# Second-half score blocks issued on the neighbouring array tiles, in turn with those of the first half

## What is computed

```python
scores = jnp.einsum('bhqd,bhkd->bhqk', q, k) / math.sqrt(D_HEAD)
scores = jnp.where(causal, neg_inf, scores)
vals, idx = jax.lax.top_k(scores, K_S)
masked = jnp.put_along_axis(jnp.full_like(scores, -jnp.inf), idx, vals, axis=-1, inplace=False)
out = jnp.einsum('bhqk,bhkd->bhqd', jax.nn.softmax(masked, axis=-1), v)
...
h = jax.nn.relu(jnp.einsum('edi,bsi->bsed', proj_in, x))
o = jnp.einsum('eid,bsed->bsei', proj_out, h)
return jnp.einsum('bsei,bse->bsi', o, gate)
...
xq = _quantize_activations(x @ H)
return jnp.einsum('bsi,oi->bso', xq, _ternary_quantize_ste(weight))
```

## Time and profile before

| | us |
|---|---|
| median of 3 runs | 622.53 |
| lowest, highest | 621.35, 623.42 |
| profiled execution, own time | 624.53 |
| its span | 622.7 |
| PE busy in the span | 553.3 (89%) |
| DVE busy | 477.5 (77%) |
| ACT busy | 387.2 (62%) |
| POOL busy | 344.3 (55%) |

### The profile page before, as it was taken

How to read it: one execution, slowest core, us unless ns; L and a number is a source line. 1 busy time by engine, 2 the same in 40 slices (tenths; PEclk the granted TensorE clock), 3 DMA queues, 4 the chain that set the end, 5 groups by cost and what they waited for, 6 DMA issues and landing times. The chain is left out here.

```text
span 622.7 us, 20334 instructions
## 1 busy us (share of the span) xinstructions
PE 553.3 (89%) x7156; PEld 478.9 (77%) x7156; DVE 477.5 (77%) x2995; ACT 387.2 (62%) x909; POOL 344.3 (55%) x336
## 2 busy tenths in 40 slices
PE   4565648999899999999999999999999999989942
PEld 3454537898788888888888888888888888878831
DVE  1898879986889978898879887988789898553213
ACT  3688558666567566766667576766575767646520
POOL 2488556753447464754556455655554656555831
PEclk9568578999999999999999999999999999999985
DMA  7244220001000200002000100020001000000000
GB/s 234 78 146 136 86 103 2 3 17 37 3 2 3 64 8 2 3 3 69 3 1 21 53 3 2 3 70 1 3 3 53 3 3 1 19 0 3 18 0 17
DMA packets 20021, 19.88 MB, mean 32 GB/s; under 512 B 1744, under 2 KB 17872, under 8 KB 19920
## 3 DMA queue, kind: packets, MB, share of 16 engines
q1 hardware_dynamic: 19920, 18.59, 9.6%
HBM read 16.49 MB, written 2.10 MB: 30 GB/s over the span
## 5 line engine op out<-in xcount | busy, mean ns | idle before, releaser
L462 POOL TENSOR_TENSOR h_lo<-h_raw,h_hi 128x512 f16<-128x512 f32 x128 | 149.5, 1169 | 158.9 <-ACT h_raw L580 158.2
L768 PE MATMUL ps_o<-w_hi,h_lo 128*128 128x256 f16 x512 | 139.8, 273 | 4.3 <-POOL h_lo L462 3.1
L752 PE MATMUL ps_z<-x1t_hi,w_lo 128*128 128x256 f16 x512 | 140.5, 274 | 0.6 <-DVE x1t_lo L910 0.6
L752 PE MATMUL ps_z<-x1t_lo,w_hi 128*128 128x256 f16 x512 | 140.3, 274 | 0.0
L752 PE MATMUL ps_z<-x1t_hi,w_hi 128*128 128x256 f16 x512 | 140.3, 274 | 0.0
L768 PE MATMUL ps_o<-w_hi,h_hi 128*128 128x256 f16 x512 | 139.5, 273 | 0.0
L768 PE MATMUL ps_o<-w_lo,h_hi 128*128 128x256 f16 x512 | 139.5, 273 | 0.0
L854 DVE MATCH_REPLACE8 taken<-next,taken 128x48 f32<-128x48 f32 (+2 forms) x576 | 127.6, 233 | 0.2
L576 ACT ACTIVATE h_hi<-ps_z 128x512 f16<-128x512 f32 x128 | 75.9, 593 | 57.9 <-PE ps_z L752 57.0
L849 DVE MAX8 next<-taken 128x8 f32<-128x48 f32 (+2 forms) x576 | 95.9, 235 | 0.1
L483 POOL TENSOR_TENSOR acc<-go_sb,acc 128x512 f32<-128x512 f32 x56 | 71.2, 1271 | 36.4 <-ACT go_sb L590 36.2
(11 more groups left out here) (106 smaller groups left out, 993.5 us busy)
## 6 DMA issues: line engine op xcount, KB each, us to landing
w_raw<-in_w1t SPq DMA_DIRECT2D x8, 512.0 KB, 3.8
w_raw<-in_w2t SPq DMA_DIRECT2D x8, 512.0 KB, 5.0
xt_sb<-in_xt SPq DMA_DIRECT2D x8, 256.0 KB, 3.3
x_sb<-in_x SPq DMA_DIRECT2D x8, 256.0 KB, 3.1
out<-out_sb SPq DMA_DIRECT2D x8, 256.0 KB, 2.1
ctx_sb<-in_ctx_w SPq DMA_DIRECT2D x8, 128.0 KB, 2.3
itok_sb<-in_itok SPq DMA_DIRECT2D x8, 128.0 KB, 2.5
wq_sb<-in_wqt SPq DMA_DIRECT2D x1, 256.0 KB, 2.9
```

Source lines behind the costliest of these rows:

```text
L462: nc.gpsimd.tensor_tensor(h_lo[:, e % 2, 2 * z:2 * z + 2, :], h_raw[:, z, :, :], h_hi[:, e % 2, 2 * z:2 * z + 2, :], ALU.subtract)\
L752: last = pe.matmul(ps_z[z][:, d * UT:(d + 1) * UT], w[:, e, c, at:at + P], x[:, c, :], start=n == 0, stop=n == len(terms) - 1)
L768: last = pe.matmul(ps_o[e % 2][:, b * D:(b + 1) * D], h[:, e % 2, c, b * SEQ:(b + 1) * SEQ], w[:, e, c, :], start=n == 0, stop=n == len(te ...
```

## The change

The loop over the blocks is turned inside out, so that a block of the first half and one of the second are issued in turn: 16, 80, 32, 96, 48, 112, 64, 128 columns. The second half's matmuls write to the output strip `STRIPS[s ^ 1]` in place of `STRIPS[s]`: strip 0 of the operands goes to output strip 1, 1 to 0, 2 to 3, 3 to 2. They are then on the array tile beside the diagonal one. The second half's mask matmuls follow to the same tiles. Since the heads of the second half now lie exchanged, two by two, in the rows of `s_sb` and of all that follows from it, `attend` takes for the second half the columns of head `h ^ SH` (`SH` is 2). Number, shape and type of all instructions stay, and so do all waits and the order on ACT, DVE, POOL and SP.

```diff
-                    for half in range(2):
-                        for i in range(HALF):
+                    for i in range(HALF):
+                        for half in range(2):
                             j = HALF * half + i
                             to = LO_FROM + score_at(j)
-                            for at in STRIPS:
-                                pe.matmul(ps_s[at, to:to + keys(j)],
+                            for s, at in enumerate(STRIPS):
+                                pe.matmul(ps_s[STRIPS[s ^ half], to:to + keys(j)],
                                           q_spread[at, k, j, :, :].rearrange("p h q -> p (h q)"),
                                           kt_sb[at, g, b * SEQ:b * SEQ + keys(j)], start=i == 0, stop=True,
                                           skip_group_check=True)
...
-                        for at in STRIPS:
-                            own = ps_s[at, to - step_by:to + (HALF - 1) * step_by].rearrange("p (i c) -> p i c", i=HALF)
+                        for s, at in enumerate(STRIPS):
+                            own = ps_s[STRIPS[s ^ half], to - step_by:to + (HALF - 1) * step_by]\
+                                .rearrange("p (i c) -> p i c", i=HALF)
...
-                                             pt_sb[:, k % 2, h, HALF * half:HALF * (half + 1), :]
+                                             pt_sb[:, k % 2, h ^ SH * half, HALF * half:HALF * (half + 1), :]
```

## The result

The median of six runs of the changed kernel is **618.5 us** (616.88 to 619.88), against 622.35 us (621.35 to 623.42, six runs) for the kernel before on the same chip: a ratio of 0.9937, with a 95% interval of 0.9918 to 0.9957. The forecast was 617.4 us in a range of 614.3 to 622.8. The sign, the range and most of the mechanism came out as written. Two steps did not: what PE keeps at tile k = 0, and the size of a block's saving. Together with two smaller errors they nearly cancelled each other. The experiments are about the two.

The account below looks back on a forecast made before the run. PE was taken as the bound from 98 to 600 us. Whole savings in 14 blocks (4.2 us), part in 5 (0.9), nothing in 6: 5.1 us off the 622.53 us median gives 617.4 us, range 614.3 to 622.8.

Parts of the forecast that it names:

- the mechanism: Score block: tiles beside the diagonal stream at once with the diagonal ones, so masks begin at 0.77 us instead of 1.06.
- what PE keeps at tile k = 0: First tile of units 3 to 7: five blocks save nothing, PE's wait at `turn_probs` growing from 0.32 to 0.62 us.
- the size of a block's saving: Each score block on PE becomes 0.30 us shorter, with bounds of 0.27 and 0.33 us.
- two smaller errors: Tile k = 3: 0.18 us kept in five blocks; first dense units: whole savings of 0.30 us at some tiles.

## What to carry to other kernels

A stretch without idle time has a fixed length only if each of its rows has the length of its equals: look for a DVE row well above its kind's median, and whether it ends just behind a row of POOL; such a row is a wait, and it may pass on a saving from elsewhere. Small matmuls on array tiles that share rows or columns but write to different PSUM banks overlap if they are issued in turn, the short ones first; new tiles without the new order gave a third of it. (Two such tiles in one bank were not run.) And what a shortened piece is worth is decided at the next wait behind it: here, piece by piece, between all and nothing of the same 0.26 or 0.35 us.

## What the runs showed of the hardware

- Tiles that share 32 rows with one tile and 32 output columns with another, and write to another bank, stream at once with them: 1152 columns a strip in 0.85 us instead of 1.11, and 0.73 with equal halves.
- PE passes over few waiting matmuls: a free tile stood idle for 226 ns behind another tile's steps, yet masks started ahead of eleven score passes that come before them in the program.
- A DVE row held by POOL shows as busy (0.84 and 0.57 us in place of 0.28, also 1.23), and ends 0.15 us after POOL's. Cutting POOL's row in two cost 0.19 us (1.35 for 1.16).
- 32 matmuls with their loads of 64 columns on two tiles take 0.90 us from first to last start, 64 with 32 columns on four tiles 0.56, for the same product.
- At the lower clock level a changed score block takes 1.435 us, at the higher one 0.848.
